# Attention scores of two heads in two 64-row halves of TensorE, wide rows in two steps, loop over key groups written out

## What is computed

```python
y = x * rsqrt(mean(x * x) + 1e-6) * rms_w
q, k, v = split(y @ w_in.T)            # 32 x 64, 8 x 64, 8 x 64
q, k = rope(q), rope(k)
qk = where(causal, q @ k.T * 64 ** -0.5, -inf)
o = softmax(qk) @ v
a = x + o @ w_out.T
x1 = layernorm(x + a)
x_q, w_q = ternary(x1, 0.33, 0.5), ternary(weight, 0.2, 0.6)
out = layernorm(x1 + x_q @ (w_q + rram_variation).T)
```

## Time and profile before

| | |
|---|---|
| timed runs, median of 3 | 1520.88 us (1519.64 to 1521.97) |
| the profiled execution, its own time | 1519.98 us |
| its span | 1518.2 us |
| PE matmul busy, share of the span | 1392.5 us, 92% |
| PE weight load busy | 1145.0 us, 75% |
| DVE busy | 1113.8 us, 73% |
| ACT busy | 1080.9 us, 71% |
| POOL busy | 837.5 us, 55% |
| mean granted TensorE clock | 0.967 |

### The profile page before, as it was taken

One profiled execution on the slowest core, in us unless ns is written; L12 is line 12 of the kernel. 1 busy time (PEld: TensorE's weight loads), 2 busy tenths in 40 slices (PEclk: granted clock), 3 DMA queues, 4 the chain that ended last, 5 costly groups with the idle time before them and its releaser, 6 DMA issues.

```text
span 1518.2 us, 30199 instructions
## 1 busy us (share of the span) xinstructions
PE 1392.5 (92%) x7472; PEld 1145.0 (75%) x7472; DVE 1113.8 (73%) x2534; ACT 1080.9 (71%) x2277; POOL 837.5 (55%) x831
## 2 busy tenths in 40 slices
PE   3489999999989998999989998999989999996785
PEld 2368887888878887888878887888878888875664
DVE  2268777877777776877777776777777778787896
ACT  3277878777777787787767787787867778784442
POOL 1365666375646666475646665475636665561243
PEclk9699999999999999999999999999999999998998
DMA  5001211021101111121101101121101101111111
GB/s 180 14 26 30 70 32 29 26 55 43 35 20 51 46 33 30 27 54 47 29 24 50 48 27 31 29 50 50 27 22 50 51 24 29 31 48 35 35 50 55
DMA packets 50534, 62.30 MB, mean 41 GB/s; under 512 B 10672, under 2 KB 31408, under 8 KB 50352
## 3 DMA queue, kind: packets, MB, share of 16 engines
q1 hardware_dynamic: 50352, 60.20, 13.8%
HBM read 34.74 MB, written 4.46 MB: 26 GB/s over the span
## 4 chain that ended last, share of the span: by engine, by line
PE 78%; issue 7%; DVE 6%; POOL 3%; ACT 2%; DMA 2%; SPq 0%; DVEq 0%; ACTq 0%; POOLq 0%
PE s L1082 18%; PE x L1106 16%; PE t L1146 15%; PE x L1130 11%; PE ot L1048 8%; PE ot L1046 8%; DMA swapped<-flat 2%; PE x L1114 1%; DVE stats L833 1%; DVE prob_lo L993 1%; PE x L1033 1%; DVE prob L912 1%; POOL flat L667 1%; POOL flat L664 1%; PE x L1088 1%
## 5 line engine op out<-in xcount | busy, mean ns | idle before, releaser
L912 DVE CUSTOM_DVE_ANT_0 prob<-s,mask 128x896 f32<-128x896 f32 (+7 forms) x512 | 382.8, 754 | 170.6 <-PE s L1082 149.9
L739 ACT ACTIVATE prob_hi<-t 128x512 fp32r<-128x512 f32 x576 | 341.3, 592 | 173.9 <-PE t L1146 143.0
L993 DVE TENSOR_TENSOR prob_lo<-t,prob_hi 128x512 fp32r<-128x512 f32 x576 | 394.0, 686 | 75.5 <-ACT prob_hi L739 69.7
L1082 PE MATMUL s<-k_t,q_t 128*128 128x512 f32 (+3 forms) x1536 | 385.0, 370 | 31.3 <-POOL q_t L680 17.7
L766 ACT ACTIVATE prob<-prob,neg_max 128x896 f32<-128x896 f32 (+7 forms) x512 | 393.4, 770 | 22.6 <-DVE neg_max L912 18.5
L1146 PE MATMUL t<-ident,prob 128*128 128x128 f32 x2304 | 350.0, 275 | 18.4 <-issue 18.4
L1146 PEld LDWEIGHTS t<-ident,prob 128*128 128x128 f32 x2304 | 289.3, 141 | 96.5 <-issue 22.2
L1082 PEld LDWEIGHTS s<-k_t,q_t 128*128 128x128 f32 x1536 | 266.0, 196 | 89.4 <-DVE neg_max L912 32.2
L1046 PE MATMUL ot<-prob_hi,v_sb 128*128 128x512 f32 x576 | 246.4, 428 | 0.0
L1048 PE MATMUL ot<-prob_lo,v_sb 128*128 128x512 f32 x576 | 231.2, 401 | 1.0 <-DVE prob_lo L993 0.9
L706 POOL TENSOR_TENSOR o_lo<-o_raw,o_hi 128x256 fp32r<-128x256 f32 x128 | 94.3, 737 | 214.2 <-ACT o_hi L819 211.4
(11 more groups left out here) (93 smaller groups left out, 1958.5 us busy)
## 6 DMA issues: line engine op xcount, KB each, us to landing
swapped<-flat SPq DMA_DIRECT2D x320, 64.0 KB, 2.0
spread<-recip_rows SPq DMA_DIRECT2D x128, 128.0 KB
recip_rows<-turned SPq DMA_DIRECT2D x512, 0.5 KB
acc<-L_attn_x SPq DMA_DIRECT2D x4, 1024.0 KB, 8.5
raw<-L_attn_w_in SPq DMA_DIRECT2D x8, 512.0 KB, 5.5
raw<-L_attn_w_out SPq DMA_DIRECT2D x8, 512.0 KB, 4.6
out<-acc SPq DMA_DIRECT2D x16, 256.0 KB, 2.0
raw<-L_attn_w_in SPq DMA_DIRECT2D x16, 128.0 KB, 6.0
```

The lines of the kernel that those rows point to most:

```text
L739: act.activation(prob_hi[:, u % 2, :], t_ps[u % 2][:, :], ACT.Copy).then_inc(prob_hi_done, 1)
L912: dve.tensor_tensor_reduce(out=prob_row(s, h), in0=s_ps[:, off:off + cols], in1=mask[:, KEYS - cols:KEYS], scale=-DH ** -0.5, scalar=3e38, ...
L993: dve.tensor_tensor(prob_lo[:, u % 2, :], t_ps[u % 2][:, :], prob_hi[:, u % 2, :].bitcast(F32), ALU.subtract).then_inc(prob_lo_done, 1)
L1082: mm = pe.matmul(s_ps[:, off + c * P:off + c * P + cols], q_t[:, h, s * P:(s + 1) * P], k_t[:, part, keys:keys + cols], start=(part == 0), ...
```

## The change

- **Scores.** `q_t` becomes `[P, 2, 2, NT * P]`: two heads of a chunk lie on the two halves of the partitions, high part and rest in two planes. An `sc` event is now one pair of heads and one stretch of up to 512 columns. It issues six matmuls with 64 rows each: hi.hi, hi.lo, lo.hi, for the head on rows 0 to 63 and the head on rows 64 to 127 in turn; each head writes its own bank. The product lo.lo is no longer made.
- **Reading.** DVE takes a row of over 512 columns in two instructions per head; the second starts from the minimum of the first (`low_max`).
- **Halves of q.** ACT writes the high parts of two heads in one copy, POOL the rests in one subtraction.
- **Loop.** All eight passes are written out; targets are constants; the separate increment behind a wait (`met`, L397) and `pool_idle` go. `opening`, the middle passes and `final` have tables of their own.
- **First pass.** Its order is a list (`FIRST`); DVE instead of POOL does rotation and rests there; the first four tiles of x are loaded and squared one by one.
- **Last pass.** A new event `fl` loads the feed-forward weights and POOL makes them ternary; POOL also makes the ternary values of the first 14 tiles, in three steps.

```diff
+SCORED = (0, 2, 4, 6, 8, 12, 16, 20, 24)
+def score_parts(s):
+    return [(pair, c) for pair in range(HG // 2) for c in range(s // HALF + 1)]
...
-        q_t = sb("q_t", [P, HG, NT * P], F32R)
+        q_t = sb("q_t", [P, 2, 2, NT * P], F32R)
+        low_max = sb("low_max", [P, HG])
...
-            one(-1, first)
-            met_counts.clear()
-            one(0, opening)
-            met_counts.clear()
-            with eng.Fori(1, LAST) as g:
-                one(g, body)
-            met_counts.clear()
-            one(LAST, final)
+            for g, plan in enumerate(plans, -1):
+                one(g, plan)
...
-            load_x(0)
+            for t in range(4):
+                sp.dma_start(acc[:, t, :], x_v[:, t, :]).then_inc(x_tile_in[t], 16)
...
-                                pool.tensor_tensor(q_t[DH:P, 2 * c, at], x[0:DH, :], q_t[0:DH, 2 * c, at].bitcast(F32),
-                                                   ALU.subtract).then_inc(part_lo, 1)
...
-                                pool.tensor_tensor(q_t[0:DH, 2 * c + 1, at], x[DH:P, :],
-                                                   q_t[DH:P, 2 * c + 1, at].bitcast(F32), ALU.subtract
+                                pool.tensor_tensor(q_t[:, c, 1, at], x, q_t[:, c, 0, at].bitcast(F32), ALU.subtract
                                                    ).then_inc(parts_done, 1)
...
-                                act.activation(q_t[0:DH, 2 * c, at], x[0:DH, :], ACT.Copy)
-                                act.activation(q_t[DH:P, 2 * c + 1, at], x[DH:P, :], ACT.Copy).then_inc(parts_hi, 1)
+                                act.activation(q_t[:, c, 0, at], x, ACT.Copy).then_inc(parts_hi, 1)
...
+                        if e[0] == "fl":
...
+                            pool.tensor_scalar(raw[:, 2, :], raw[:, 0, :], TH_W, SC_W, ALU.is_gt, ALU.mult
+                                               ).then_inc(tern_step, 1)
...
+                            pool.tensor_scalar(tern_tile(t), acc[:, t, :], TH_X, None, ALU.is_gt).then_inc(below_done, 1)
+                            pool.tensor_scalar(below_tile(t), acc[:, t, :], -TH_X, None, ALU.is_lt).then_inc(below_done, 1)
+                            pool.wait_ge(below_done, 2 * t + 2)
+                            pool.tensor_tensor(tern_tile(t), tern_tile(t), below_tile(t), ALU.subtract
...
+                            for a in range(2):
+                                h = 2 * pair + a
+                                least = neg_max[:, kk % 4, h:h + 1] if c == s // HALF else low_max[:, h:h + 1]
+                                dve.tensor_tensor_reduce(out=prob_row(s, h)[:, c * BANK:c * BANK + cols],
+                                                         in0=s_ps[:, a * BANK:a * BANK + cols],
+                                                         in1=mask[:, seen:seen + cols], scale=-DH ** -0.5,
+                                                         scalar=low_max[:, h:h + 1] if c else 3e38,
+                                                         op0=ALU.add, op1=ALU.min, accum_out=least
...
-                                for part in range(2):
-                                    mm = pe.matmul(s_ps[:, off + c * P:off + c * P + cols], q_t[:, h, s * P:(s + 1) * P],
-                                                   k_t[:, part, keys:keys + cols], start=(part == 0), stop=(part == 1))
+                            wait(pe, max_done, g, 2 * SCORES_MADE, 2 * n)
+                            for q_part, k_part in ((0, 0), (0, 1), (1, 0)):
+                                for a, rows in enumerate((slice(0, DH), slice(DH, P))):
+                                    mm = pe.matmul(s_ps[:, a * BANK:a * BANK + cols],
+                                                   q_t[rows, pair, q_part, s * P:(s + 1) * P],
+                                                   k_t[rows, k_part, keys:keys + cols],
+                                                   start=(q_part == k_part), stop=(q_part == 1))
```

More of the change, by code:

```diff
@@ L64, in __init__, with number @@
         self.behind = [[] for _ in range(slots)]
-    def number(self, pads=0):
-        self.pads = pads
-        self.x = {("pad", n): n for n in range(pads)}
+    def number(self):
+        self.x = {}
         for u in range(len(self.ahead)):
@@ L136, in put @@
         placed.append((at, len(placed), e))
-    for b, s in [(0, s) for s in range(2, NT)] + [(1, s) for s in range(NT)] + [(2, 0), (2, 1)]:
-        if last and b == 2:
-            continue
-        scores, exps, norm, spread = SCORES[b * NT + s - 2]
-        for h in range(HG):
-            put(scores[h], ("sc", b, s, h))
+    for b, s in [(0, s) for s in range(2, NT)] + [(1, s) for s in range(NT)] + (
+            [] if last else [(2, 0), (2, 1)]):
+        scores, exps, norm, spread = at_pass["SCORES"][b * NT + s - 2]
+        for at, (pair, c) in zip(scores, score_parts(s)):
+            put(at, ("sc", b, s, pair, c))
         for h in range(HG):
@@ L147, in body_plan @@
         put(spread, ("rs", b, s))
-    for n, (chunks, turn) in enumerate((FIRST_HALF,) + PROJECT):
+    for n, (chunks, turn) in enumerate(at_pass["PROJECT"], 0 if opening else 1):
         b, half = divmod(n + 1, 2)
-        if n == 0 and not opening or b == 2 and last:
-            continue
         for c, places in zip((2, 0, 1), chunks):
@@ L180, in body_plan @@
             continue
-        for kind, lag in zip(("oe", "on", "oh", "op"), OUTPUT[b * NT + s + 1]):
+        for kind, lag in zip(("oe", "on", "oh", "op"), at_pass["OUTPUT"][b * NT + s + 1]):
             put(STEPS * end + lag, (kind, b, s))
@@ L311, in seq_block @@
         x_in = [sem(f"x_in{n}") for n in range(4)]
+        x_tile_in = [sem(f"x_tile_in{n}") for n in range(4)]
         ffn_in = [sem(f"ffn_in{n}") for n in range(2)]
@@ L410, in wait_x_free @@
             n, past, back = plan.x[e] - RING, plan, 0
-            if n < plan.pads:
+            if n < 0:
                 if plan is first:
                     return
-                n = n if n < 0 else n - RING
                 past, back = plan.past, 2
-                n += past.uses
-                while n >= len(past.x):
-                    n -= RING
             kind, *what = list(past.x)[n]
-            assert len(what) >= 2 or not back or kind == "norm"
             if kind == "pj":
@@ L431, in wait_x_free @@
             elif kind == "w":
-                wait(eng, win_done, g, 4, 4 + what[0] + 1)
+                wait(eng, win_done, g, 4, 4 + what[0] + 1 - 2 * back)
             elif kind == "wo":
-                wait(eng, wout_done, g, 2, what[0] + 1)
+                wait(eng, wout_done, g, 2, what[0] + 1 - back)
             elif kind == "fw":
@@ L444, in chunk, with scored @@
             return 3 * (2 * b + half) + PLACE[c]
+        def scored(b, s, pair=0, c=0):
+            return b * SCORED[NT] + SCORED[s] + pair * (s // HALF + 1) + c
+        SCORES_MADE = 2 * SCORED[NT]
         def unit_of(u):
@@ L657, in one @@
                             x, turned_x = flat[rows, n % 2, :], swapped[rows, n % 2, :]
-                            if plan is first or plan is opening and half:
+                            if plan is opening and half:
                                 pool.wait_ge(table_in[half], 32)
+                                pool.wait_ge(parts_done, 3)
                             wait(pool, swapped_in[n % 2], g, swaps(10), swaps(n))
-                            met(pool)
                             pool.tensor_tensor(turned_x, turned_x, sin_sb[rows, q_half(half)], ALU.mult
@@ L1150, in one @@
                     events(plan.behind[u])
-                    if 0 < u <= plan.units or u == 0 and plan in (body, final):
+                    if 0 < u <= plan.units or u == 0 and plan not in (first, opening):
                         values(u - 1)
```

301 lines of the change are left out of this document (140 added, 161 removed), and 84 rows, old and new, of tables (EARLY, FIRST, OUTPUT, PROJECT).

## The result

| | before | after |
|---|---|---|
| timed runs, median | 1521.43 us (4 runs) | 1537.38 us (4 runs) |
| ratio | | 1.0102, 95% interval 1.0084 to 1.0119 |
| span of the profiled execution | 1518.2 us | 1532.4 us |
| mean granted clock of TensorE | 0.967 | 0.978 |

The change makes the kernel 1% slower; 7% faster was forecast. First the page of the changed kernel: its head, the busy time of each engine, and the chain that ended last by engine and by line.

The account below looks back on a forecast made before the run. PE was taken as the bound, full but for 9 us a pass. From 1520 us, scores -33.6, loop -32, waits and registers -3, first pass -20 and last pass -18 gave 1413 us, range 1350 to 1500.

Parts of the forecast that it names:

- slower: the switch drains PE and uncovers the load: Rival on score steps: 1576 us at 0.27 us a switch; chance 0.09 for over 0.19, 0.07 for 0.12 to 0.19.
- Scores: forecast -33.6: Score products on PE: 70.6 us saved, less 37 us for 742 changes of shape, net -33.6 us.
- The saving of 70.6: Score steps: one product's price saved in each, 4.4 us a group times 16, if halves run side by side.
- the lower end: Price of a change of shape on PE: lower bound nothing; 0.05 us was taken, nearer to this end.
- My upper bound: Price of a change of shape on PE: a tail of 0.16 and an unhidden load of 0.11, 0.27 us.
- The loop: forecast -32: Five jumps back: each hole of 3.8 us and 2.6 us from the half clock go, 32 us.
- Waits and registers: -3: Register steps and increments behind waits go: 3 us counted, between 0 and 10.
- DVE's 60 us "beside PE": Split rows on DVE: 60 us more work, costed at nothing beside PE; without the cover up to 60.
- First pass: forecast -20: First pass: new order, earlier second q copy, rotation and subtraction on DVE save 20 us, from 10 to 28.
- the three shares of the forecast: First pass: 3.6 us from POOL's steps on DVE, 8 from the order, perhaps 8 from the earlier second copy.
- Last pass: forecast -18: Last pass: ternary feed-forward weights on POOL and earlier, tiles' ternary steps off DVE; 18 us saved, from 5 to 30.

Follow-up runs that it names:

- Run 8: Kernel before with only its loop over six passes written out: 1490.71 us, 0.9788.
- 1: Changed kernel with three full-height products a score step in place of six 64-row ones, heads summed, so another output: 1447.56 us, 0.9515.
- 2: Changed kernel with before's score products, four at full height in steps of two heads, and q laid out as before: 1535.77 us, 1.0083.
- Run 12: Changed kernel with its tables, first and last pass, but scores one head a step, full height, rows unsplit: 1553.79 us.
- run 9: Kernel before with its loop written out and the change's first pass, scores, tables and last pass as before: 1464.52 us, 0.9624.
- 16: Changed kernel with its own tables and load times, but last-pass weights and tiles made ternary on DVE: 1524.87 us, 1.0027.
- 17: Kernel of run 9 with the feed-forward weights loaded and made ternary on DVE earlier: 1451.89 us, 0.9542.
- 7: Changed kernel with the three products of one head issued, then the other's three, instead of taking turns: 1537.88 us.

## Why the prediction was wrong

The rival "slower: the switch drains PE and uncovers the load" came true, at 0.195 us a switch, just above the 0.19 from which it was said to decide. That part of it had a chance of 0.09. With this one term put right the sum gives 1413 + 108 = 1521, no change; the rest, up to 1537, is in the main the last pass.

**Scores: forecast -33.6, the step that failed.** The saving of 70.6 was right: spacings fall by 8.8 us a pass, halves and loads run side by side. The switch was priced 0.05 and measured 0.195: 145 us instead of 37, so the scores cost 74 us net where they were to give 33.6. I took the lower end because the earlier trace rows show a change of kind for free, but that is a change between two full-height kinds, whose loads stay covered; it was no row for a change of shape. My upper bound, a tail of 0.16 and a load of 0.11, named both parts rightly; the timeline has some 0.09 and 0.10 of them. With nothing nearer in the trace, the upper bound had a mechanism for each of its parts and the lower end had none.
The Trainium skill (TensorEngine Tiling (Array Packing), Tiling Modes) states that changing the tiling mode drains TensorE. The trace agrees: the first load of the new shape starts with its product and not under the product before, and the runs give 0.195 us a switch.

**The loop: forecast -32, right.** Run 8 gives 31, for the jumps and the register steps of the loop together.

**Waits and registers: -3, not measured by itself.** The working has some 2.4 us a pass left beside the jump; its own figures, 169.7 - 160.5 - 6.4, give 2.8. Run 8, without jumps, leaves 2.6, so the register steps gave next to nothing; the change leaves 1.4 beside the switches. Yet the term at nothing, DVE's 60 us "beside PE", hid something: with the switches gone (1 and 2) 8 to 10 us a pass are left over, and PE waits, in 1 for DVE and in 2 for DVE and POOL. Run 12 shows that the split rows are not their cause in this order; the order itself is. The waits are for the banks of scores in the main. That the order fits the durations of the halves and not those of plain products is my reading of it; no run tests durations apart from order. That is how taking the halves out gave only 90 us (1) or nothing (2), and why the price of the halves must be read with each in its own order: 171.5 against 163.1 is +8.4 a pass, which is -8.8 of spacings, +18.4 of 94 switches, and -1.2 of waits.

**First pass: forecast -20, from 10 to 28; measured -25.7** in the trace, -26 by run 9. The size is right, near the upper end; 9 takes order, loads and DVE's part together, so how the three shares of the forecast (3.6, 8 and 8 us) came out is not known. The opening pass is 5.3 us longer, where a middle pass against that of 8 is 8.4 longer.

**Last pass: forecast -18, measured +17.2, the second step that failed.** By the prices its products are 8.4 us shorter and its 82 switches 16.0 longer: +8. POOL's part is 7 to 12 (16). What is left, up to 2 us, lies between order and waits and wasn't taken apart. I priced POOL's slowness with its step of two inputs, 1.28 us, and its single-input comparisons are 1.5 and, with two operations, 1.9 us; three steps of them stand in every tile's path. The wait of 18 us that I saw in the earlier trace rows was real, and 12.6 us of it are to be had (17), by an earlier start on DVE and not by another engine.

**Sum.** Scores +145 - 71, loop -31, first pass -26, POOL's part of the last pass +7 to +12: +24 to +29 us on 1521, and +16 was measured. The 1.2 us a pass by which the change waits less than 8 are 10 us over eight passes and about close the gap.

## What to carry to other kernels

A change of the matmul's shape costs PE a hold and an uncovered weight load each time: here 0.195 us, as much as 0.8 of a product of 512 columns. A step here saved one spacing, 0.233 us, and paid 0.39 for its two changes. Halves pay only where more is saved between two changes than that (no run here tried longer steps). Where the order is written by hand, try each part of a change in an order that was made for it, and take the parts that stand alone first: a loop written out, a first pass and four earlier weights gave 4.6% here, while the whole change lost 1%.

## What the runs showed of the hardware

Products on the other 64 rows start ahead of products issued before them. In 7 each head's three were issued together, and they still ran in pairs, whose starts lie 10 ns apart in the median of the records. In the change the last-issued product of a step, which carries the semaphore's increment, started before its partner in 50 of the 384 steps, by up to 22 ns.
The Trainium skill (TensorE: Matmul & The Clock Gate, Part 3) says that matmuls start and end in the order of the program. These starts do not agree with it, and the measurement decides. The ends in the records are modelled, so no run here shows whether an increment on the last one is safe.

GpSimd is slower with one input than with two: a comparison of a 128x512 float32 tile takes 1.52 us, with a second operation 1.93, but a subtraction of two tiles 1.28. VectorE takes 0.49 for the comparison and 0.69 for two inputs, so 3.1 and 1.9 times less.

A pass of PE lost 10.5 us of 163 to another order of the same instructions (8 against 12), with ACT, the busiest engine beside PE, at 79% in the shorter pass.
